# Second cross-attention of a perceiver: key scores as three products of split operands, and the value projection moved ahead of the own scores

## The reference

```python
x = x + _L1_xattn_ref(_layernorm(x, axis=-1), ctx_2048, L1_xattn_w_qkv, L1_xattn_w_proj, L1_xattn_b_proj)
```

## Time and profile before

| | |
|---|---|
| median of 3 runs | 468.68 us (468.66 to 470.43) |
| profiled execution, first to last instruction | 467.3 us |
| PE busy | 449.3 us, 3500 records |
| ACT busy | 240.2 us |
| DVE busy | 256.2 us |
| POOL busy | 123.5 us |
| mean granted TensorE clock | 0.996 of full speed |

### The profile page before, as it was taken

One profiled execution on the slowest core, in us unless ns is written; L12 is line 12 of the kernel. 1 busy time (PEld: TensorE's weight loads), 2 busy tenths in 40 slices (PEclk: granted clock), 3 DMA queues, 4 the chain that ended last, 5 costly groups with the idle time before them and its releaser, 6 DMA issues.

```text
span 467.3 us, 8504 instructions
## 1 busy us (share of the span) xinstructions
PE 449.3 (96%) x3500; PEld 385.6 (83%) x3500; DVE 256.2 (55%) x455; ACT 240.2 (51%) x439; POOL 123.5 (26%) x113
## 2 busy tenths in 40 slices
PE   8999999999999999999987999999999999999997
PEld 7887989989897989899966677998666779778797
DVE  2656223245426232232045788985567765469996
ACT  2577334264445343242113777762788764347872
POOL 1110000002000500000021277966920000019795
PEclk9999999999999999999999999999999999999999
DMA  8925400005200020000039999998000039264000
GB/s 281 412 96 194 180 2 1 1 0 183 89 0 1 13 90 1 1 1 1 1 121 426 362 294 337 420 389 361 2 1 1 2 119 418 96 269 181 0 1 13
DMA packets 13191, 62.65 MB, mean 134 GB/s; under 512 B 1365, under 2 KB 3813, under 8 KB 7392
## 3 DMA queue, kind: packets, MB, share of 16 engines
q1 hardware_dynamic: 11072, 54.31, 30.8%
q0 software_dynamic: 2080, 7.80, 4.7%
HBM read 61.97 MB, written 0.13 MB: 133 GB/s over the span
## 4 chain that ended last, share of the span: by engine, by line
PE 76%; DVE 6%; ACT 5%; DMA 5%; POOL 3%; issue 3%; SPq 0%; DVEq 0%; ACTq 0%; POOLq 0%
PE W L1590 20%; PE W L1546 15%; PE W L1749 7%; PE W L1830 4%; DMA ctxmem<-units_dram 4%; PE W L1884 4%; PE W L1929 3%; PE W L1563 3%; POOL w_lo L552 3%; PE W L1947 2%; PE W L1612 2%; PE W L1469 2%; DMA fixed<-units_dram 1%; PE W L1871 1%; PE W L1498 1%
## 5 line engine op out<-in xcount | busy, mean ns | idle before, releaser
L1590 PE MATMUL W<-probs_turned_hi,ctx_split_hi 128*128 128x256 f32 x256 | 72.8, 285 | 2.6 <-issue 2.5
L1590 PE MATMUL W<-probs_turned_hi,ctx_split_lo 128*128 128x256 f32 x256 | 72.4, 283 | 0.0
L1590 PE MATMUL W<-probs_turned_lo,ctx_split_hi 128*128 128x256 f32 x256 | 72.4, 283 | 0.0
L1024 DVE TENSOR_TENSOR probs_turned_lo<-W,probs_turned_hi 128x512 fp32r<-128x512 f32 x32 | 20.6, 686 | 64.9 <-ACT probs_turned_hi L693 64.9
L1590 PEld LDWEIGHTS W<-probs_turned_hi,ctx_split_hi 128*128 128x128 f32 x256 | 49.1, 192 | 3.8 <-issue 3.3
L561 POOL TENSOR_TENSOR small<-small,const 128x1 f32<-128x1 f32 (+2 forms) x10 | 7.0, 697 | 163.4 <-DVE small L1097 75.3
L1590 PEld LDWEIGHTS W<-probs_turned_lo,ctx_split_hi 128*128 128x128 f32 x256 | 49.1, 192 | 0.2
L1590 PEld LDWEIGHTS W<-probs_turned_hi,ctx_split_lo 128*128 128x128 f32 x256 | 49.1, 192 | 0.0
L712 ACT ACTIVATE pbuf<-W,small 128x1024 f32<-128x1024 f32 x16 | 17.9, 1116 | 59.6 <-DVE small L1044 59.6
L552 POOL TENSOR_TENSOR w_lo<-arena,w_hi 128x320 fp32r<-128x320 f32 x30 | 41.3, 1390 | 26.1 <-ACT w_hi L634 25.6
L552 POOL TENSOR_TENSOR w_lo<-ctxmem,w_hi 128x320 fp32r<-128x320 f32 (+1 forms) x30 | 46.3, 1568 | 5.1 <-ACT w_hi L634 4.6
(11 more groups left out here) (403 smaller groups left out, 907.6 us busy)
## 6 DMA issues: line engine op xcount, KB each, us to landing
arena<-units_dram SPq DMA_DIRECT2D x22, 1024.0 KB, 11.5
ctxmem<-units_dram SPq DMA_DIRECT2D x16, 1024.0 KB, 15.2
fixed<-units_dram SPq DMA_DIRECT2D x6, 1024.0 KB, 6.1
pbuf<-ctx_dram POOLq DMA_DIRECT2D x4, 512.0 KB, 6.3
ctxmem<-ctxT_dram SPq DMA_DIRECT2D x8, 256.0 KB, 11.8
ctxmem<-ctx_dram SPq DMA_DIRECT2D x2, 1024.0 KB, 14.6
scr<-ctx_dram POOLq DMA_DIRECT2D x3, 512.0 KB, 4.2
vecs<-vectors_dram POOLq DMA_DIRECT2D x1, 1040.0 KB, 7.6
```

The source lines that it names most:

```text
L1024: dve.tensor_tensor(PT[1][at], bank(4 + c).rearrange("p (t m) -> p t m", t=4), f32(PT[0][at]), ALU.subtract).then_inc(ev("pl_sb"), 1)
L1590: mm = pe.matmul(ps, CXN[a][:, t, c * P:(c + 1) * P], PT[z][:, t, :], start=(t == 0 and n == 0), stop=(t == KEYT - 1 and n == 2))
```

## The change

- sim1 makes three pairs of products in place of one pair, in the order of TERMS. The high and the low part of the queries are the two tiles of QZ, those of the keys lie in the four weight slots of WH and WL (keys_split), one slot per four rounds. own_scores makes three products for each one, 24 per batch, from QZ and the two tiles of K1.
- ACT makes the high parts of the keys (keys_hi, four casts of 128x1024), three ahead of and one behind its copy of the transposed x. GpSimd makes the low parts (keys_lo, four subtractions of 128x1024), and does m1e0's and m1e1's split behind the bias rows and the scaled weight, each slot when its four rounds of scores are done (sim1_done).
- DVE writes the high queries in one operation per batch and the low ones in two per batch (queries_lo), those of batch 1 behind the first maximum, and the low part of the own keys (k1_lo).
- The own values (v1) are projected into bank 6 right behind sim1(0), and are copied by ACT ahead of the own scores; stay_warm there has 2 products in place of 5. The waits for ctxT_in move to ACT, that for ctxN_in behind own_scores(1).

```diff
+        QZ = [cut(acts, 1024 * n, 4, B, 2, NQ) for n in range(2)]
+        K1 = [cut(acts, 5376, 4, TOK), cut(acts, 2048, 4, TOK)]
+        def keys_split(part, m):
+            return w_slot(part, MOE0 + m).rearrange("p (b k) -> p b k", b=B)
...
+                    def keys_lo(m):
+                        pool.wait_ge(ev("keys_hi"), m + 1)
+                        pool.tensor_tensor(keys_split(1, m), KEYS[:, :, m, :], f32(keys_split(0, m)), ALU.subtract)\
+                            .then_inc(ev("keys_lo"), 1)
+                    keys_lo(0)
+                    keys_lo(1)
                     for m in range(4):
                         pool.memset(probs1[:, m, NCTX + NQ * (1 - m % 2):NCTX + NQ * (2 - m % 2)], 0.0)\
                             .then_inc(ev("pads_zero"), 1)
-                    for p in range(MOE0, MOE0 + SLOTS):
-                        keep_w(0, p)
-                        keep_w(1, p)
+                    keys_lo(2)
+                    keys_lo(3)
...
+                    for m in range(SLOTS):
+                        pool.wait_ge(ev("sim1_done"), 4 * (m + 1))
+                        keep_w(0, MOE0 + m)
+                        keep_w(1, MOE0 + m)
...
+            def keys_hi(m):
+                if m == 0:
+                    act.wait_ge(ev("ctxT_in"), 16 * B * len(ROWS_OF))
+                act.wait_ge(ev(slot_free(MOE0 + m)[0]), slot_free(MOE0 + m)[1])
+                act.copy(keys_split(0, m), KEYS[:, :, m, :]).then_inc(ev("keys_hi"), 1)
+            for m in range(3):
+                keys_hi(m)
             keep_xT(bank(4))
+            keys_hi(3)
             act.wait_ge(*made("k1_ps"))
-            act.copy(K1, bank(7).rearrange("p (m t) -> p m t", m=4)).then_inc(*tick("k1_sb"))
+            act.copy(K1[0], bank(7).rearrange("p (m t) -> p m t", m=4)).then_inc(*tick("k1_hi"))
+            act.wait_ge(*made("v1_ps"))
+            act.copy(vsb[:, :], bank(6)[:, 0:DIM]).then_inc(ev("v_sb"), 1)
...
+            def queries_hi(b):
+                dve.tensor_tensor(QZ[0][:, :, b], bc(own_queries(b), 2, 2), bc(bc(hmask, 1, 4), 3, NQ), ALU.mult)\
+                    .then_inc(ev("qz_hi"), 1)
+                dve.wait_ge(ev("qz_hi"), b + 1)
+            def queries_lo(b):
+                for h in range(2):
+                    dve.scalar_tensor_tensor(out=QZ[1][:, :, b, h, :], in0=own_queries(b), scalar=hmask[:, h:h + 1],
+                                             in1=f32(QZ[0][:, :, b, h, :]), op0=ALU.mult, op1=ALU.subtract)\
+                        .then_inc(ev("qz_lo"), 1)
+            queries_hi(0)
+            queries_lo(0)
+            queries_hi(1)
+            dve.wait_ge(*made("k1_hi"))
+            dve.tensor_tensor(K1[1], bank(7).rearrange("p (m t) -> p m t", m=4), f32(K1[0]), ALU.subtract)\
+                .then_inc(*tick("k1_lo"))
...
                     step(dve.tensor_reduce(mx[:, r % 2:r % 2 + 1], W[r % 2][:, :], AX_X, ALU.max))
+                    if r == 0:
+                        queries_lo(1)
...
+                if r % 4 == 0:
+                    pe.wait_ge(ev("keys_hi"), r // 4 + 1)
...
-                for kh in range(2):
-                    at = 64 * (j % 2) + 32 * kh
-                    mm = pe.matmul(W[r % 2][:, kh * 512:(kh + 1) * 512],
-                                   QZ[at:at + 32, j // 2, b].rearrange("p h q -> p (h q)"),
-                                   KEYS[at:at + 32, b, j // 2, :], start=True, stop=True)
+                for n, (a, z) in enumerate(TERMS):
+                    if z == 1 and r % 4 == 0:
+                        pe.wait_ge(ev("keys_lo"), r // 4 + 1)
+                    if a == 1 and r < 2:
+                        pe.wait_ge(ev("qz_lo"), 2 * (r + 1))
+                    for kh in range(2):
+                        at = 64 * (j % 2) + 32 * kh
+                        mm = pe.matmul(W[r % 2][:, kh * 512:(kh + 1) * 512],
+                                       QZ[a][at:at + 32, j // 2, b].rearrange("p h q -> p (h q)"),
+                                       keys_split(z, j // 2)[at:at + 32, b, :], start=(n == 0), stop=(n == 2))
...
             sim1(0)
-            pe.wait_ge(*made("k1_sb"))
+            for k in range(KT):
+                mm = pe.matmul(bank(6)[:, 0:DIM], xT[:, k, :], wx[:, k, 512:768], start=(k == 0), stop=(k == KT - 1))
+            mm.then_inc(*tick("v1_ps"))
+            pe.wait_ge(*made("k1_lo"))
             own_scores(0)
             sim1(1)
+            pe.wait_ge(ev("v_sb"), 2)
             own_scores(1)
+            pe.wait_ge(ev("ctxN_in"), 16 * B)
             pe.wait_ge(ev("self_sb"), 2)
-            stay_warm(4, 5)
-            for k in range(KT):
-                mm = pe.matmul(bank(4)[:, 0:DIM], xT[:, k, :], wx[:, k, 512:768], start=(k == 0), stop=(k == KT - 1))
-            mm.then_inc(*tick("v1_ps"))
+            stay_warm(4, 2)
```

More of the change, by code:

```diff
@@ L239 @@
     "scalar_made": [
-        "sqk_ready", "qr_sb", "sqq_ready", "qTA_sb", "kTA_sb", "simA_exp", "ptA_sb", "gT_sb", "xat_dup", "k1_sb", "rb0_sb", "rb1_sb", "expA", "diag_ready", "dte",
+        "sqk_ready", "qr_sb", "sqq_ready", "qTA_sb", "kTA_sb", "simA_exp", "ptA_sb", "gT_sb", "xat_dup", "k1_hi", "rb0_sb", "rb1_sb", "expA", "diag_ready", "dte",
         "dtl", "cums", "ex0_ready", "ex1_ready", "th45", "z_tanh", "ysq0_ready", "ysq1_ready", "sct", "pq_sb", "km_sb", "vmT_sb",
@@ L243 @@
     "vector_made": [
-        "null_sb", "nv_ready", "kn_ready", "simA_max", "probsA", "hm_ready", "gT_lo", "sums0_ready", "sums1_ready", "o1_ready1", "o1_ready0",
+        "null_sb", "nv_ready", "kn_ready", "simA_max", "probsA", "hm_ready", "gT_lo", "k1_lo", "sums0_ready", "sums1_ready", "o1_ready1", "o1_ready0",
         "dtn_ready", "xp_sb", "dtA_ready", "xc0", "xc45", "xc1", "M0_ready", "M1_ready", "ya0_ready", "ya1_ready", "scz", "scb_ready",
@@ L406, in half_in @@
             return unit(SPLIT[p // 2])[:, (p % 2) * HALF:(p % 2 + 1) * HALF]
-        QZ = cut(scr, 0, 4, B, 2, NQ)
+        QZ = [cut(acts, 1024 * n, 4, B, 2, NQ) for n in range(2)]
         WDUP = cut(scr, 2048, KT, 2, 4, P)
         PT1 = [cut(scr, 2048 + 1152 * n, 9, TOK) for n in range(2)]
-        SELF, K1 = cut(scr, 4352, B, PAIRS, NQ), cut(scr, 5376, 4, TOK)
+        SELF = cut(scr, 4352, B, PAIRS, NQ)
+        K1 = [cut(acts, 5376, 4, TOK), cut(acts, 2048, 4, TOK)]
         PV = cut(ctxmem, (NB + NC) * UNIT, ROWT, P)
@@ L837, in _ @@
                     if r == 0:
-                        act.wait_ge(*made("v1_ps"))
-                        act.copy(vsb[:, :], bank(4)[:, 0:DIM]).then_inc(ev("v_sb"), 1)
                         keep_own(1, 0)
@@ L1192, in _, with own_queries @@
             dve.wait_ge(*made("q1_ps"))
[L1193 to L1196, removed]
+            def own_queries(b):
+                return bank(5).rearrange("p (m t) -> p m t", m=4)[:, :, b * NQ:(b + 1) * NQ]
+            def queries_hi(b):
[13 more added lines that the diff above has]
+                .then_inc(*tick("k1_lo"))
             of_half = "p (b i j) -> p i j b"
@@ L1876, in sim1 @@
                 b, j = r % 2, r // 2
+                if r % 4 == 0:
+                    pe.wait_ge(ev("keys_hi"), r // 4 + 1)
                 if r < 2:
-                    pe.wait_ge(ev("qz_ready"), r + 1)
+                    pe.wait_ge(ev("qz_hi"), r + 1)
                 if r >= 2:
                     pe.wait_ge(ev("exp1_done"), r - 1)
-                for kh in range(2):
-                    at = 64 * (j % 2) + 32 * kh
-                    mm = pe.matmul(W[r % 2][:, kh * 512:(kh + 1) * 512],
-                                   QZ[at:at + 32, j // 2, b].rearrange("p h q -> p (h q)"),
-                                   KEYS[at:at + 32, b, j // 2, :], start=True, stop=True)
+                for n, (a, z) in enumerate(TERMS):
[8 more added lines that the diff above has]
+                                       keys_split(z, j // 2)[at:at + 32, b, :], start=(n == 0), stop=(n == 2))
@@ L1887, in sim1 @@
                 mm.then_inc(ev("sim1_done"), 1)
-            pe.wait_ge(ev("ctxT_in"), 16 * B * len(ROWS_OF))
-            pe.wait_ge(ev("ctxN_in"), 16 * B)
             def own_scores(b):
-                pe.wait_ge(ev("qz_ready"), B)
+                pe.wait_ge(ev("qz_hi"), B)
+                pe.wait_ge(ev("qz_lo"), 2 * (b + 1))
                 for j in range(PAIRS):
                     m, at = j // 2, 64 * (j % 2)
-                    mm = pe.matmul(bank(SELF_BANK[b][j % 2])[:, m * NQ:(m + 1) * NQ],
-                                   QZ[at:at + 32, m, b].rearrange("p h q -> p (h q)"),
-                                   K1[at:at + 32, m, b * NQ:(b + 1) * NQ], start=True, stop=True)
+                    for n, (a, z) in enumerate(TERMS):
+                        mm = pe.matmul(bank(SELF_BANK[b][j % 2])[:, m * NQ:(m + 1) * NQ],
+                                       QZ[a][at:at + 32, m, b].rearrange("p h q -> p (h q)"),
+                                       K1[z][at:at + 32, m, b * NQ:(b + 1) * NQ], start=(n == 0), stop=(n == 2))
```

2 lines of the change are left out of this document (removed).

## The result

| | before | after |
|---|---|---|
| median of 4 runs, same chip | 469.44 us (468.66 to 470.43) | 478.32 us (477.16 to 479.30) |
| profiled execution, own time | not given | 478.06 us |
| its span | 467.3 us | 476.2 us |
| mean granted TensorE clock | 0.996 | 0.982 |

The ratio is 1.0188, with a 95% interval of 1.0146 to 1.0229. The changed kernel is slower by 8.9 us. The forecast was 467.9 in a range of 465.3 to 471.3: the result lies outside the range, and the time rose where a small fall was forecast. (Medians in this document are of all runs, ratios leave out the runs that took over 1.5% longer than the fastest of their kernel.)

A forecast was written before the change was run, and what follows sets the result against it. It took TensorE alone to bound the loop, 2.96 us a round without waits. Loop -2.3, start +0.2 and clock +1.3 sum to -0.8 us; from 468.7 that gives 467.9 us, range 465.3 to 471.3.

The forecast's parts named there:

- sim1 in the loop, -2.3 us: Score products in the loop: sim1 0.88 us for 1.06, 0.18 us less per round, thirteen on the chain.
- the two bounds: Limits for sim1's three pairs in the loop: 0.84 us (-2.9 in all) to 1.08 us (+0.3).
- loads not hidden: Rival, sim1 in the loop: every pair pays its weight loads, sim1 1.08 us, total 470.5 us; chance 0.12.
- row groups in turn: Rival, sim1: fp32r products on different rows don't run side by side, sim1 1.57 us, about +8.2, 477; chance 0.10.
- The own scores, 0.065 each: Ahead of the loop: 24 fp32r records a batch at 0.065 us, 1.56 us a batch, about 0.6 more.
- The start as a whole, +0.2: Ahead of the loop: time won by moved own values and fewer warming records is used up by added products.
- DVE there, "Hidden": Ahead of the loop: DVE's own-key part ends at 323.1 before own_scores(0) at 323.6; low queries hidden by 0.4 us.
- GpSimd, "4 x 2.35 from 316.5 ... Nothing": Ahead of the loop: four low key parts of 2.35 us, first ready at 318.9 for sim1(0) at 321.7; no cost.
- The clock, +1.3: Ahead of the loop: one 3.4 us drop to half clock doubles the products under it.
- half for longer: Rival: the wait for the first exponential holds the clock at half another 3.4 us, +1.3 more, 469.2 to 470; chance 0.13.
- Expert split and power request: Behind the last sim1: GpSimd's split ends by about 369, power request at 378.84, some 7 us of cover; no cost.

The follow-up runs named there:

- e4: e1 with eight warming products in place of two ahead of the loop; 468.58 us, ratio 0.9968.
- e9: Kernel before with four GpSimd casts of 128x1024 (one SBUF input) added where keys_lo stands in the changed kernel; 470.54 us, one run.
- e6: e5 with eight warming products in place of two; 472.15 us, ratio 1.0038.
- e12: Kernel before with eight warming products in place of five; 470.96 us, ratio 1.0024.
- e8: e5 with five warming products in place of two; 468.10 us, ratio 0.9949.
- e1: Changed kernel with GpSimd's first keys_lo held until DVE is past its small operations behind the layer norm; 473.24 us, ratio 1.0045.
- e2: Kernel before with two GpSimd subtractions of 128x1024 from SBUF added where keys_lo stands in the changed one; 472.97 us, ratio 1.0045.
- e3: Changed kernel with all three sim1 products of one key half issued before those of the other; 478.08 us, two runs, ratio 1.0165.
- e5: e1 with the first exponential put ahead of ACT's third copy of own scores, two warming products; 472.13 us, ratio 1.0019.
- e10: e1 with five warming products in place of two; 473.86 us, ratio 1.0032.

## Why the prediction was wrong

*sim1 in the loop, -2.3 us*: **right in mechanism, a little large**. sim1 takes 0.90 us for the forecast 0.88, the round 2.80 for 2.78. From sim1(4) on it saved 1.7 us, and another 0.4 from sim1(2) to sim1(4) where the clock stayed (4.84 us in e4, 5.20 before). It lies between the two bounds, and both rivals on the array (loads not hidden, row groups in turn) fell: a pair costs 0.24 us, under the 0.29 from which the change would have lost. The rule of the Trainium skill ("TensorE: Matmul & The Clock Gate", Part 3) that a load overlaps only products of another row group is not borne out here: the loads at 350.69 stand under products of their own rows.

*The own scores, 0.065 each*: **right**. 19 records took 1.23 us at 330.77.

*The start as a whole, +0.2*: **right against this profile** (7.37 against 7.42 us), **for a reason that the forecast missed**. The 7.42 of before held a fall of the clock; at full clock the same stretch is 5.82 us (e9). Against that the new start is 1.6 us longer, and it is what eats the loop's 1.7. With the clock whole in both, the stage is 48.8 us after (e4, e6) and 50.0 before with as much warming (e12); at five products it is 49.4 (e9 without the 0.6 us that its casts cost hn). So the change wins 0.6 to 1.2 us in the stage. The runs at a clock of 1.00 say a little more: medians of 468.0 for e4 and 467.3 for e8, against 469.6 and 469.1 for the kernel before beside them.

*DVE there, "Hidden", and GpSimd, "4 x 2.35 from 316.5 ... Nothing"*: **this step failed**. The forecast cost each engine's added work on that engine alone and looked for semaphores between them. There are none between keys_lo and hn, and still hn waited for keys_lo: +1.95 us, and behind it a clock at half for the projections, +2.6. e1 takes both away, e2 puts them on the kernel before. Without the overlap DVE's added work is hidden as forecast: in e1 the own-key part ends at 325.38, and own_scores(0) begins at 325.92. The forecast even had the collision in its numbers: it let GpSimd start at 316.5, and hn began at 316.48 in the trace of before. A warning stood there too. Timelines of GpSimd and DVE in its feed-forward layer:

```profile
302.88 3.01 POOL L552 TENSOR_TENSOR w_lo<-ctxmem,w_hi 128x320 fp32r<-128x320 f32 x2
...
304.11 2.55 DVE L987 TENSOR_TENSOR w_lo<-ctxmem,w_hi 128x704 fp32r<-128x704 f32 x2
```

GpSimd's subtraction takes 1.5 us for 320 columns there; the earlier trace rows show 2.35 for 1024, which would be 0.73 for 320 (an estimate), and the shortest of that size in the same trace took 0.88. Two engines that slow each other with the same kind of operation, and no wait between them: that row, read against its own size, would have told it.

*The clock, +1.3*: **right in kind, too small**. The forecast took one fall as long as the 3.4 us of before; it lasted 9.9, and sim1(2) to sim1(4) took 3.7 us more. The rival "half for longer" had named this (+2.6 in all) with a chance of 0.13, still 1.1 short. The first fall, over the projections, was in no case. Why the second lasts so much longer than that of before stays open.

*Expert split and power request*: **right**. The split ended at 380.35 and the request came at 387.61.

*The range.* It had no case in which two added pieces hit each other. The stage's +6.8 us from the median of 468.7 would have given 475.5; the 2.2 ahead of it belong to no step of the change that I can name. Whether they are chance stays open: all four runs of the changed kernel lie above 477.

## What to carry to other kernels

Before moving elementwise work to GpSimd, list what DVE does from SBUF to SBUF in the same microseconds, and put no long GpSimd instruction right ahead of one that TensorE waits for: hn of 0.41 us took 2.42, and the cure was one semaphore (4.9 us from hn to sim1(0)). To see whether two engines block each other, compare an operation's time per column where they overlap and where they don't. And ask of a baseline interval whether it already held a fall of the clock: a change that is measured against it looks better there than it is.

## What the runs showed of the hardware

- A 128x4 operation on DVE took 2.37 us behind a GpSimd subtraction of 128x1024, 0.89 behind a GpSimd cast, and 0.17 alone (e1); a reduction (0.16) and a product that reads PSUM (0.69) under the same subtractions did not stretch.
- Products of fp32r on different 32-row groups ran side by side at 0.24 us a pair of 512 columns, also when issued three and three (e3).
- The granted clock fell under a TensorE that had been busy for 6.00 of 6.00 us with products of 32 rows for the most part (e5), and whether it falls differs from run to run of one kernel. Once down it stayed at half for 3.4 us (before), 9.9 (after), 10.3 (e1), 13.5 (e5, e10) and 15.1 (e8).
- The same kernel's mean clock and time go together: e4 took 466.8 to 468.8 us at 1.00, 472.8 to 477.8 at 0.989 and below.
